# Layer 2 of a four-layer kernel: another order in the front, four banks for it, and two steps moved in the scan loop

## The reference, cut to what matters

```python
xc = conv1d(x_main, conv_w, k=3, per channel) + conv_b     # x_main, z = split(x @ W_in.T): 256 channels each
x_main = silu(xc)
dbc = x_main @ W_x.T                     # 64 columns for dt, 16 for B, 16 for C
dt = softplus(dbc[:, :64] @ W_dt.T + b_dt)
for each of 16 states n:                 # h over the 512 tokens
    h_t = exp(dt_t * A_n) * h_(t-1) + dt_t * x_t * B_t[n];   y_t += h_t * C_t[n]
y = (y + x_main * D_param) * silu(z);  mixer = layernorm(y @ W_out.T + x) * gamma + beta

logits = silu(x @ rw1 + rb1) @ rw2 + rb2            # router
w = softmax of the two best logits, 0 elsewhere
ffn = x + sum_e w[:, e] * (silu(x @ we1[e] + be1[e]) @ we2[e] + be2[e])
```

## Time and profile before

| | us |
|---|---|
| runs (3) | 1404.35, 1404.84, 1404.96; median 1404.84 |
| the profiled execution | 1417.23 |
| its span | 1415.5 |
| VectorE busy in the span | 997.0 (70%) |
| TensorE busy in the span | 1155.0 (82%) |
| ScalarE, GpSimd busy | 761.7, 615.9 |

### The profile page before, as it was taken

One profiled execution on the slowest core, in us unless ns is written; L12 is line 12 of the kernel. 1 busy time (PEld: TensorE's weight loads), 2 busy tenths in 40 slices (PEclk: granted clock), 3 DMA queues, 4 the chain that ended last, 5 costly groups with the idle time before them and its releaser, 6 DMA issues. The chain is left out here.

```text
span 1415.5 us, 21028 instructions
## 1 busy us (share of the span) xinstructions
PE 1155.0 (82%) x7010; PEld 812.6 (57%) x7010; DVE 997.0 (70%) x2280; ACT 761.7 (54%) x1584; POOL 615.9 (44%) x607
## 2 busy tenths in 40 slices
PE   3999999998888786377966887888887778988885
PEld 1455665664564575266844555555555555777774
DVE  2476677669787654567737989989989997634445
ACT  1456556555545445244437686586767674344442
POOL 3244444544348824443101533633633753136661
PEclk9999999999999898588978998998999999789997
DMA  7400000000000033810000000000000000001113
GB/s 174 117 1 1 1 1 1 1 1 1 1 8 24 30 89 102 253 35 16 1 12 0 1 1 1 1 1 0 1 1 1 1 1 14 18 17 39 40 38 105
DMA packets 54443, 40.71 MB, mean 29 GB/s; under 512 B 13185, under 2 KB 46687, under 8 KB 54337
## 3 DMA queue, kind: packets, MB, share of 16 engines
q1 hardware_dynamic: 40994, 27.58, 6.8%
q0 software_dynamic: 4544, 9.32, 2.4%
q10 hardware_dynamic: 8800, 2.48, 0.9%
HBM read 26.32 MB, written 13.04 MB: 28 GB/s over the span
## 5 line engine op out<-in xcount | busy, mean ns | idle before, releaser
L780 POOL TENSOR_TENSOR PR<-PR,R 128x512 f32<-128x512 f32 (+3 forms) x128 | 160.6, 1266 | 231.7 <-DVE R L1275 231.2
L1980 POOL TENSOR_TENSOR YY<-YY,H 128x512 f32<-128x512 f32 x120 | 164.3, 1392 | 187.6 <-DVE H L2430 187.6
L410 PE MATMUL banks<-XT,we 128*128 128x128 f32 (+1 forms) x568 | 175.2, 440 | 11.9 <-ACT HH L2252 10.5
L1074 ACT ACTIVATE PR<-banks,NM 128x257 f32<-128x257 f32 (+3 forms) x256 | 132.4, 527 | 94.8 <-DVE NM L1247 93.0
L410 PEld LDWEIGHTS banks<-we,HH 128*128 128x128 f32 x1024 | 145.1, 205 | 35.4 <-issue 30.2
L2422 DVE TENSOR_TENSOR_SCAN H<-wide,H 128x1024 f32<-128x1024 f32 x64 | 164.4, 2568 | 0.2
L410 PE MATMUL banks<-we,HH 128*128 128x128 f32 x1024 | 145.5, 289 | 0.0
L410 PE MATMUL banks<-BCR,SEL 96*128 96x512 f32 x128 | 68.2, 535 | 76.4 <-DVE H L2430 65.1
L2252 ACT ACTIVATE HH<-banks,be1f 128x512 f32<-128x512 f32 x128 | 84.1, 687 | 83.5 <-PE banks L410 82.6
L410 PEld LDWEIGHTS banks<-XT,we 128*128 128x128 f32 x568 | 90.4, 202 | 65.3 <-issue 43.4
L410 PEld LDWEIGHTS banks<-PTS,V 128*64 128x64 f32 x1152 | 66.4, 139 | 84.1 <-issue 53.7
(11 more groups left out here) (564 smaller groups left out, 2447.5 us busy)
## 6 DMA issues: line engine op xcount, KB each, us to landing
xsort<-zrow SPq DMA_DIRECT2D x1, 3072.0 KB, 13.9
XS<-xsort SPq DMA_DIRECT2D x12, 256.0 KB, 2.9
ysort<-PTS SPq DMA_DIRECT2D x12, 256.0 KB, 2.2
pj_stage<-in_L_ffn_w_proj SPq DMA_DIRECT2D x1, 2048.0 KB, 12.0
we<-in_L_ffn_we SPq DMA_DIRECT2D x1, 2048.0 KB
we<-yrows SPq DMA_DIRECT2D x8, 256.0 KB, 5.4
xrows<-XN SPq DMA_DIRECT2D x4, 256.0 KB, 3.5
out<-XN SPq DMA_DIRECT2D x4, 256.0 KB, 2.3
```

Of the source, the lines that this page charges most:

```text
L410: return nc.tensor.matmul(o, l, r, start=start, stop=stop)
L780: last = nc.gpsimd.tensor_tensor(p, p, R[:, T * q + t, :].unsqueeze(2).to_broadcast([P, 2, w]), ALU.mult)
L1074: nc.scalar.activation(PR0[:, q % 2, s, OFF[t]:OFF[t] + w], ps2(n)[:, s, SLOT[t]:SLOT[t] + w], ACT.Exp, bias=NM[:, m, s:s + 1], accum_out= ...
L1980: nc.gpsimd.tensor_tensor(YY[:, m, :], YY[:, m, :] if n else XD[m], H[:, k % 4, m, :], ALU.add).then_inc(ya, 1)
```

## The change

For batch 0 alone, four banks are used: r1 in bank 5, c's and dt's halves in 6 and 7, the rest in bank 0, and each use waits for the readers that it needs (`first_needs`) and not for the reader of the use before. TensorE's order becomes xnt, c 0, c 1, r1, dbc, dt 0, dt 1, logits, the first row of B, and then the hidden products; wT waits last, after the first hidden products and rows. ScalarE does the silus of the convolution ahead of the router's, and the shares' exponential and the first four hidden silus after the first decays. VectorE takes logits and choice after the first two `inputs`, and `share(0)` after scan(0). The router's hidden tile of batch 0 gets a buffer of its own (XN), since XNT now holds dbc at that time. In the loop, `gate` goes ahead of the four hidden silus in step 1 of a batch, and `correction` goes from step 11 to step 12, behind the scan.

```diff
@@ -1890,9 +1890,14 @@
                 uses[key] = len(uses)
             front_order = {4: (("xnt",),), 5: (("r1",),), 6: (("logits",),), 7: (("c", 0), ("c", 1)), 8: (("dbc",),),
                            9: (("dt", 0), ("dt", 1)), 14: (("wT",),)}
-            for n in range(NS):
-                for key in front_order.get(n, ()):
-                    use(key[0], 0, *key[1:])
+            for key in (("xnt",), ("c", 0), ("c", 1), ("r1",), ("dbc",), ("dt", 0), ("dt", 1), ("logits",), ("wT",)):
+                use(key[0], 0, *key[1:])
+            first_bank = {("r1",): 5, ("c", 0): 6, ("c", 1): 7, ("dt", 0): 6, ("dt", 1): 7}
+            first_needs = {("c", 0): ("xnt", 0), ("c", 1): ("xnt", 0), ("r1",): ("xnt", 0), ("dbc",): ("c", 0, 1),
+                           ("dt", 0): ("dbc", 0), ("dt", 1): ("dbc", 0), ("logits",): ("dbc", 0)}
+
+            def bank_for(kind, b, *m):
+                return PS[:, first_bank.get((kind, *m), 0) if b == 0 else 0, :]
             spare_at = {}
             for k in range(NK):
                 b, n = divmod(k, NS)
@@ -1938,7 +1943,7 @@
                 DT = feats[:, :, :].rearrange("p (i m) s -> p i m s", i=2)
                 DA = wide[:, :, :, :]
                 HH3 = wide[:, 0:2, :, :].rearrange("p i m s -> p (i m) s")
-                H1 = XNT[:, :]
+                H1 = [XN[:, :, :].rearrange(flat)] + [XNT[:, :]] * (B - 1)
                 DBC = XNT[0:96, :]
                 wrow = DA[:, 0, :, :].rearrange("p m s -> p (m s)")[:, 0:768]
 
@@ -2013,10 +2018,12 @@
                     def _(pe):
                         def spare(key):
                             kind, b = key[0], key[1]
-                            i = uses[key]
-                            if i:
-                                pe.wait_ge(m0, i)
-                            o = PS[:, 0, :]
+                            needs = first_needs.get((kind, *key[2:])) if b == 0 else None
+                            if needs:
+                                pe.wait_ge(m0, read(*needs))
+                            elif uses[key]:
+                                pe.wait_ge(m0, uses[key])
+                            o = bank_for(*key)
                             xt = XT[:, b % 2, 1:S + 1]
                             if kind == "xnt":
                                 for t in range(T):
@@ -2031,7 +2038,7 @@
                             elif kind == "logits":
                                 pe.wait_ge(m0, read("r1", b))
                                 for t in range(T):
-                                    last = mm(o[:, t * NE:(t + 1) * NE], H1[:, t * P:(t + 1) * P], rw2[:, 0:NE])
+                                    last = mm(o[:, t * NE:(t + 1) * NE], H1[b][:, t * P:(t + 1) * P], rw2[:, 0:NE])
                             elif kind == "c":
                                 m = key[2]
                                 if b == 0 and m == 0:
@@ -2068,6 +2075,8 @@
                                 pe.wait_ge(hs, g - 2)
                             if e == 0 and i == 0:
                                 pe.wait_ge(m0, read("xnt", b))
+                            if g == 2:
+                                pe.wait_ge(m0, read("r1", 0))
                             mm(PS[:, 3 + g % 3, :], we1[:, e, i * P:(i + 1) * P], XT[:, b % 2, 1:S + 1]).then_inc(hp, 1)
 
                         def chunk(g):
@@ -2099,23 +2108,18 @@
                             mm(PS[:, 2, :], SEL[:, NS + n:NS + n + 1].to_broadcast([96, P]), BCR[:, b % 2, :]).then_inc(cp, 1)
 
                         pe.wait_ge(s_w2, 32)
-                        spare(("xnt", 0))
-                        spare(("r1", 0))
-                        spare(("logits", 0))
-                        spare(("c", 0, 0))
+                        for key in (("xnt", 0), ("c", 0, 0), ("c", 0, 1), ("r1", 0), ("dbc", 0), ("dt", 0, 0), ("dt", 0, 1),
+                                    ("logits", 0)):
+                            spare(key)
+                        b_row(0)
                         hidden(0)
-                        spare(("c", 0, 1))
                         hidden(1)
-                        spare(("dbc", 0))
                         hidden(2)
-                        spare(("dt", 0, 0))
-                        hidden(3)
-                        spare(("dt", 0, 1))
-                        b_row(0)
                         b_row(1)
                         c_row(0)
+                        b_row(2)
+                        hidden(3)
                         spare(("wT", 0))
-                        b_row(2)
                         for k in range(NK):
                             chunk(2 * k)
                             if k:
@@ -2193,14 +2197,14 @@
                             act.wait_ge(mp, read("r1", b))
                             if b:
                                 act.wait_ge(bcr, b)
-                            nc.scalar.activation(H1, o, ACT.Silu, bias=rb1[:, :]).then_inc(m0, 1)
+                            nc.scalar.activation(H1[b], bank_for("r1", b), ACT.Silu, bias=rb1[:, :]).then_inc(m0, 1)
 
                         def x_silu(b, m):
                             act.wait_ge(mp, read("c", b, m))
                             if b:
                                 act.wait_ge(yi, 2 * b)
                                 act.wait_ge(dtx, b)
-                            nc.scalar.activation(XM[:, m, :], o, ACT.Silu, bias=convb[:, m:m + 1]).then_inc(m0, 1)
+                            nc.scalar.activation(XM[:, m, :], bank_for("c", b, m), ACT.Silu, bias=convb[:, m:m + 1]).then_inc(m0, 1)
 
                         def dbc(b):
                             act.wait_ge(mp, read("dbc", b))
@@ -2210,12 +2214,14 @@
                             act.wait_ge(mp, read("dt", b, m))
                             if b:
                                 act.wait_ge(dts, b)
-                            nc.scalar.activation(DT[:, b % 2, m, :], o, ACT.Relu, bias=bdt[:, m:m + 1])
-                            nc.scalar.activation(E[:, m, :], o, ACT.Abs, bias=bdt[:, m:m + 1]).then_inc(m0, 1)
+                            nc.scalar.activation(DT[:, b % 2, m, :], bank_for("dt", b, m), ACT.Relu, bias=bdt[:, m:m + 1])
+                            nc.scalar.activation(E[:, m, :], bank_for("dt", b, m), ACT.Abs, bias=bdt[:, m:m + 1]).then_inc(m0, 1)
 
                         def dt_exp(b):
                             act.wait_ge(m0, read("dt", b, 1))
                             nc.scalar.activation(E, E, ACT.Exp, scale=-1.0).then_inc(dte, 1)
+
+                        def share_exp(b):
                             act.wait_ge(shifted, b + 1)
                             nc.scalar.activation(PR[:, :, 0:NE], PR[:, :, 0:NE], ACT.Exp).then_inc(expd, 1)
 
@@ -2266,21 +2272,22 @@
 
                         apply_in(0)
                         turn_in(0)
+                        x_silu(0, 0)
+                        x_silu(0, 1)
                         router(0)
-                        x_silu(0, 0)
-                        hidden(0)
-                        x_silu(0, 1)
-                        hidden(1)
                         dbc(0)
-                        hidden(2)
                         dt_parts(0, 0)
-                        hidden(3)
                         dt_parts(0, 1)
                         dt_exp(0)
                         dt_log(0)
                         d_term(0)
                         decays(0)
                         decays(1)
+                        share_exp(0)
+                        hidden(0)
+                        hidden(1)
+                        hidden(2)
+                        hidden(3)
                         store_wT(0)
                         for k in range(NK):
                             b, n = divmod(k, NS)
@@ -2294,11 +2301,11 @@
                                 dt_parts(b + 1, 0)
                             if n == 13:
                                 z_silu(b, 0)
+                            if n == 1 and b:
+                                gate(b - 1)
                             if n % 2 and k + 1 < NK:
                                 for i in range(4):
                                     hidden(2 * k + 2 + i)
-                            if n == 1 and b:
-                                gate(b - 1)
                             if n == 3 and more:
                                 apply_in(b + 1)
                             if n == 5 and b:
@@ -2316,6 +2323,7 @@
                                 dt_parts(b + 1, 1)
                             if n == 10 and more:
                                 dt_exp(b + 1)
+                                share_exp(b + 1)
                             if n == 12 and more:
                                 dt_log(b + 1)
                             if n == 13:
@@ -2485,19 +2493,22 @@
                             row = wrow[:, 384 * m:384 * (m + 1)].rearrange("p (e k) -> p k e", k=3)
```

(10 more changed lines are left out.)

## The result

The changed kernel took 1389.78 us (median of 4 runs, 1388.58 to 1392.78) against 1404.9 for the kernel before on the same chip (4 runs, 1404.35 to 1406.78): ratio 0.9887, 95% interval 0.9865 to 0.9909, so 15.1 us less. The forecast was 1392.9, 11.9 less, with a range of 1388.5 to 1400.

The account below looks back on a forecast made before the run. VectorE, busy 93% of layer 2's scan loop, and its waits bound the kernel, with a serial chain in the front. Front -3.0, gate -9.2 and correction +0.3 sum to -11.9 us: 1404.84 becomes 1392.9, range 1388.5 to 1400.

Parts of the forecast that it names:

- front kept: Ahead of the first scan: biases(0) starts 3.3 us earlier, of which 3.0 taken; bounds 5.0 and -2.
- gate: Step 1 of a batch: gate ahead of the hidden silus removes 9.2 of 9.7 us of VectorE's waits; bounds 6.5 and 9.7.
- correction: Loop step 11: share takes over the correction's wait for the exponential; +0.3 us for three batches, bounds -5.6 and +1.5.
- Front, the chain: Ahead of the first scan engines work one after another; c0 starts 5.08 us earlier, the exponential of E 7.4.
- 1.3 us bound: Convolution's products in the front: the clock rising half way through c0 instead of at its end gives about 1.3 us.
- two more table loads: ScalarE in the front: 1.28 us each, hidden before scan(2) with 1.3 us to spare; otherwise 2.56 us count.
- TensorE is late at chunk(0): Front: wT waits for share with chunk(0) queued behind it, so chunk(0) starts at 759.7, only 2.6 us earlier.
- a later rise of the clock: From chunk(0) to the bias products: rise some 1.7 us later at half speed, 0.85 us lost.
- the difference carried over: Whole program: the runs' median, 12.4 us below the profiled execution, keeps that difference unchanged, giving 1392.9 us.
- the front's upper bound: Front's gain at biases(0) is 5.0 us if TensorE is not late; used for the range's low end.
- The slower rival: Loop: TensorE becomes the bound if its mean clock falls under 0.77; at 0.74 the time is 1412 us; chance 0.03.
- The Trainium skill's warning: Front: the number of slow starting matmuls differs between runs, so the gain would differ by up to 2.5 us.

Follow-up runs that it names:

- the gate alone: Kernel before with only the gate put ahead of the four hidden silus in step 1 of a batch: 1395.34 us, ratio 0.9922.
- the front alone: Changed kernel with gate and correction back in their old places, run in two sets: 1407.3 us, ratio 1.0; then 1399.64 us, ratio 0.9957.
- the two parts together: Changed kernel with the correction back in step 11 ahead of share, front and gate kept: 1405.08 us against 1421.63, ratio 0.9889.
- The second profile of before: Kernel before, unchanged, run and profiled once more: 1405.22 us, ratio 0.999; layer 2 took 483.46 us.
- the second set: Runs on another chip with the kernel before beside them at 1421.63 us; the unchanged changed kernel took 1402.43 us there, ratio 0.9879.
- the half-done move: Kernel before with only the correction moved from step 11 to step 12, behind scan(12), share left in step 11: 1405.21 us, ratio 0.9997.
- the second instruction: Changed kernel with share of the next batch also moved to step 12, behind the correction: 1385.13 us against 1406.19, ratio 0.9849.

## Why the prediction was right, by its own steps

| term | predicted | measured |
|---|---|---|
| silu of c1 | 735.0 | 734.17 |
| exponential of E | 743.3 | 742.44 |
| scan(0) | 755.7 (5.8 earlier) | 755.0 (6.53 earlier) |
| chunk(0) | 759.7 | 758.99 |
| biases(0) | 769.1, idle 1 to 2 | 767.31, idle 0.56 |
| front kept | 3.0 | 5.1 at scan(3), 3.6 at scan(13) |
| gate | 9.2 | 9.2 by the profile pair; 9.6 by the runs of the gate alone |
| correction | +0.3 | nothing measurable (0.9997; 0.9879 beside 0.9889) |
| sum | -11.9 | -15.1 |

- **Front, the chain.** Each link came within 0.9 us. The sum took the clock's rise at the end of c0. It came inside c0: 7.10 us for twelve passes, where six at half clock and six at full would be 5.34 + 2.84 = 8.2 (granted clock 0.50 in the slice from 732, 0.63 in that from 733, 1.00 from 734). This was its 1.3 us bound, nearly. The two more table loads stayed hidden, as the prediction had it: from scan(0) to biases(0) VectorE has no idle time but the 0.56.
- **Front, what is kept.** This is the term that was mis-sized. The chain said that TensorE is late at chunk(0) (right: VectorE idles 0.56 for the bank) and that a later rise of the clock costs 0.85 more inside the chunks. In fact chunk(0) to the end of the bias products took 8.28 us, less than the 8.81 before: 1.1 us of the difference lie here, 0.7 in the earlier chain.
- **And where it is kept.** The prediction carried the front's gain through to the end. It had no term for the slow hidden product of batch 0, which cost 1.5 us at scan(13) in after; what was left there, 3.6, is near the 3.0 by two errors that stand against each other. For the front alone the gain at each scan was 5.26 at scan(3), 3.95 at scan(13), 1.58 at scan(19) and -0.41 at the last one. The gate's wait at half clock ate most of it. With the gate moved there is no such wait. That fits the 16.6 us of the two parts together, where alone they gave 0 to 6.5 and 9.6; but 6.5 and 9.6 add up to 16.1, so the runs don't show that the parts need each other.
- **Gate.** Each mechanism was as written: nothing takes the place of the wait but small ones for TensorE (1.27 us for the Wout product after batch 0, of which 0.87 comes back; 0.81 at step 39; 0.80 for the bias bank of batch 3). In the pair, the three steps with a gate gain 3.57, 4.57 and 1.02 us, 9.16 in sum. What the prediction didn't know is that 9.7 is the low end of what this wait takes: 9.7 to 17.5 over six profiles, 12.4 on average. That taking it away is worth more than the 9.2 is likely but not shown: the gate alone gave 9.6, with an interval from 7.6 to 14.5.
- **Correction.** This was right, at its own place: share takes over the wait, 7.1 for 5.6.
- **The last step, the difference carried over.** The profiled execution was 12.4 us above the median for a reason that the prediction couldn't name. The second profile of before names the place: the part behind layer 2 took 200.4 us there and 214.82 in the first, 14.4 less. Carried over unchanged, the difference did no harm.
- **The range.** The measured 1389.78 lies in the stated range of 1388.5 to 1400, but not in the 1390.5 to 1395.5 that the forecast itself was given, and 15.1 us is more than the front's upper bound and the whole gate together (5.0 + 9.7 = 14.7, so 1390.1). The low end of 1388.5 is 1.6 us below what it is said to be made of, and no term accounts for these. That the number fell inside is in part luck.
- **The slower rival.** TensorE did not become the bound: the mean clock from 758 to 1190 was 0.91 in after. Its reason, that the clock falls wherever TensorE idles, is too strong. TensorE idled 2.44 us ahead of the row product at 1096.03 in before, and the clock was granted at 1.00 before and after; in the front alone it idled as long ahead of the one at 869.12, and the products behind it ran at 0.50.

By layer 2 alone the change is worth 9.6 us in the first pair, and 13.1 against the second profile of before. The runs say 15.1, and 19.2 in the second set (17.2 by its ratio). What lies between, 2 us and more, is not settled: there are traces of two executions of the kernel before and two of the changed one, and none of the other timed executions.

The Trainium skill's warning, which the prediction weighed at the front, holds in the loop. "TensorE: Matmul & The Clock Gate", Part 1, says of a kernel's start that the number of slow matmuls differs from run to run. The traces show the like in mid-kernel: the waits behind the same hidden products were 5.83, 5.82 and 1.81 us in one execution and 5.82 to 5.83 three times in another of the same kernel. At the front, where the prediction weighed it, they show next to none: the twelve passes of c0 and c1 took 6.94 to 7.10 us in all eight profiles of the new front.

## What to carry to other kernels

When a wait ends behind products of TensorE, its length is no constant: read it in several executions and with the granted clock of the stretch ahead of it, before it is priced; an instruction that needs nothing from those products belongs ahead of them. When a move only hands a wait to the next instruction on the queue, move that one too: here the half-done move gave 0, and with the second instruction layer 2 was 10.8 us shorter in the profiles and the time some 4 to 5 us in the runs. And before a difference of two profiles is explained, cut both spans at marks that the change can't touch: here 18 of 24 us lay outside it.

## What the hardware showed that was not expected

- **One kernel, two clocks at the same instruction.** With no change in the program, TensorE's stretch ahead of the gate was granted 0.50 or 1.00, and the waits were 5.8 or 1.8 us. TensorE was busy through all of each stretch (4.96 of 4.96, 5.96 of 5.96 and 3.31 of 3.31 us); at the lower clock its four hidden products took 3.78 us where they took 1.99. Other places were the same in every execution of an order, as the slow hidden product of batch 0.
- **Two rhythms of the part behind layer 2.** Over 13 profiles it took 195.5 to 200.5 us in eight and 209.9 to 214.8 in five; in one set all four kernels had the long one, and there the kernel before took 1421.63 us instead of 1405. In the long execution of before VectorE waited 30.9 us in 13 places at one copy. All five long executions have this wait, 28.9 to 32.6 us, and none of the eight short ones:
```profile
DVE YO L3040 <- remote: 30.9, 13, 3.0
```
What sets it was not tried, and it is open.
- **The scan's time depends on its company.** In after it took 2.29 us at 758.29, with GpSimd idle, and 3.16 at 766.89, when GpSimd's additions of 765.40 still had 1.0 us to go. Over the 13 profiles, the 397 scans of layer 2 with no work of GpSimd beside them took 2.27 to 2.29 us, and those with 1.0 or 1.1 us of its additions beside them 3.14 to 3.25. And a small operation of GpSimd took 2.11 us beside the scan of 775.77, where the same one took 0.23 at 725.46 with VectorE idle. This is read from the traces and was not tried by itself.
```profile
725.46 0.23 POOL L381 TENSOR_SCALAR rstd<-mv 128x4 f32<-128x4 f32 x1 [0.41 <-DVE mv L390]
...
765.40 2.50 POOL L1985 TENSOR_TENSOR YY<-SA,H 128x512 f32<-128x512 f32 x2 [36.60 <-DVE H L2438]
...
766.89 3.16 DVE L2430 TENSOR_TENSOR_SCAN H<-wide,H 128x1024 f32<-128x1024 f32 x1
...
775.94 2.11 POOL L381 TENSOR_SCALAR rstd<-mv 128x4 f32<-128x4 f32 x1 [1.40 <-DVE mv L390]
```
So a shift of one of the two engines also changes the length of the other's work, here by up to 0.9 us a scan.
